# Norm products of the odd graphs moved from ScalarE to GpSimd, and the lists of the first and last slots in another order

## The chip, the cores and the metric

The kernel runs on one core of a Trainium2 chip. The metric is the device time of one execution in microseconds; before the change it was run three times. The five engines are TensorE (PE, matmuls; PEld its weight loads), VectorE (DVE), ScalarE (ACT), GpSimd (POOL) and SyncE (SP), which here issues all DMAs.

## The reference

Two layers act on 128 graphs of 128 nodes with 512 features each. Cut to what matters:

```python
# layer 0, 8 heads of 64
h = relu(layernorm(x))
m = h @ map_w.T + map_b
n = heads(m) / max(norm(heads(m)), 1e-8)
cos = n @ n.T                       # per head
keep_edge = cos > 0.1               # a 128 x 128 mask per head
q, k = heads(m @ q_w.T + q_b), heads(m @ k_w.T + k_b)
p = softmax(mask(q @ k.T / 8, adj))
a = keep_edge * p
x = x + relu((a @ heads(h @ gcn_map_w.T + gcn_map_b)) @ gcn_W.T / (a.sum(-1) + 1))
# layer 1, 4 heads of 64
h = relu(layernorm(x))
x = x + (softmax(mask(h@Wq @ (h@Wk).T / 8, adj)) @ (h@Wv)) @ Wo + bo
```

## The kernel before

The test `cos > 0.1` is made without a division: with N_i and N_j the norms of two nodes in one head, the product of m_i and m_j is compared with 0.1 N_i N_j. That second product, 8 heads of 128 x 128 in float32, is the tile `least`. It is built from `norm` (a column of norms for each head, with the 0.1 in it) and `norm_n` (the norms spread along the free dimension of all partitions by a DMA through `norm_d`). This work is called `threshold`. In the kernel before, ACT makes it with eight activations of 128 x 128 (L951), each with one column of `norm` as its scale; only for the very last graph GpSimd makes it in one instruction (`last_threshold`, L788). DVE then subtracts `least` from the cosines in PSUM (`above`, L1299), and after the exponentials sets to zero what is not above zero (`gate`, L1305).

All products are made in float16 pairs: a tile X is split into an upper part (ACT copies it to float16) and a lower part (POOL or DVE subtracts the upper part from X), and TensorE multiplies upper by upper, upper by lower and lower by upper. `e_upper`/`e_lower` do this for the attention weights of layer 0, `p1_lower` for the softmax weights of layer 1, `m_upper`/`m_lower`, `h1_upper`/`h1_lower` and so on for the others.

The work is a software pipeline over slots, one for each graph, written out by hand: each engine has its own list of calls for an odd slot and for an even slot, and special lists for the first slots (`n == 0`, `n == 1`, `n == 2`) and the last ones (called z, a, b, ... for graphs 125, 126, 127 and the slots after them). An engine runs its list strictly in order, and semaphores tie the lists together. In one slot different graphs are at different stages: slot n holds the scores of graph n, the features of n+1 or n+2, and layer 1 of the graphs n-1 to n-5. Two slots, an even one and an odd one, make a pair, after which the pattern repeats.

What stands around the change, in a pair of slots:

- ACT, even slot: `threshold(n)`, `scores_exp(n)` (eight exponentials with row sums, L940), `l1_exp` of one graph, `e_upper`, `m_upper`, `l1_exp` of another, `squares`, `v_upper` ("va"), `lv_upper`, `threshold(n+1)`, `h1_rows` and `h1_upper` (layer 1's normalised rows, L1007 and L1015), `v_upper` ("vb"). Odd slot: `x_rows` (L1022 and L1027), `scores_exp`, `o1_upper`, `qk_upper` twice, `e_upper`, and so on to `h1_rows`, `h1_upper`.
- POOL, even slot: `h1_lower`, `v_lower`, `keep_row`, `block_mask`, `result_base` (L715), `p1_lower` (L728), `e_lower` (L733), `m_lower` (L796), `p1_lower`, `norm_l1` (the reciprocal root and the shift of layer 1's normalisation, last instruction L809, for which `h1_rows` waits), `norm_l0` (the same of layer 0 for two graphs, last instruction L822, for which `x_rows` waits). Odd slot: `x_lower`, `o1_lower` (L722), `norm_rows` (L782), `e_lower`, `result_base`, `norm_l1` and others.
- DVE, odd slot: `scores_mask` (L1282, and the row maxima L1292 for which `scores_exp` waits), `above`, `gate`, then `o1_rows` (L1416), which frees the PSUM bank into which TensorE writes the next layer 1 queries (`lqk_part`, matmuls at L1903 with `w_lq`).

The first slots also split layer 1's four weights: ACT makes the upper parts (`l1_weights_upper`, L1165), DVE the lower ones (`l1_weights_lower`, L1711), and TensorE waits for them with `lw_done` before their first use.

Of the kernel before, what the change touches and what calls it, by code (L numbers as in the profile page):

```python
# [170 lines left out]
def build(nc, x, adj, map_w, map_b, q_w, q_b, k_w, k_b, gcn_map_w, gcn_map_b, gcn_W, Wq, Wk, Wv, Wo, bo, out):  # L171
# [15 lines left out]
    with ExitStack() as ctx:  # L187
# [494 lines left out]
        def _(pool):  # L682
# [101 lines left out]
            def last_threshold(s):  # L784

                pool.wait_ge(norm_in[1], 16 * (B // 2))
                pool.wait_ge(lowered, B - 1)
                nc.gpsimd.tensor_tensor(least[:, :, :], norm_n[:, 1].rearrange("p n h -> p h n"),  # L788
                                        norm[:, H:2 * H].unsqueeze(2).broadcast_to([P, H, P]),
                                        ALU.mult).then_inc(threshold_done, 1)  # L790
# [33 lines left out]
            def slot(s):  # L824
# [16 lines left out]
                elif s.n == 0:  # L841
                    v_lower(s)
                    keep_row(s)
                    block_mask(s)
                    m_lower(s)
                    norm_l0(s)
                    e_lower(s)
                elif s.n == 2:
                    h1_lower(s)
                    m_lower(s)  # L850
                    v_lower(s)
                    keep_row(s)
                    block_mask(s)
                    e_lower(s)
                    norm_l1(s)
                    norm_l0(s)
                else:
                    h1_lower(s)
                    v_lower(s)
                    keep_row(s)  # L860
                    block_mask(s)
                    result_base(s)
                    p1_lower(s, 4)
                    e_lower(s)
                    m_lower(s)
                    p1_lower(s, 3)
                    norm_l1(s)
                    norm_l0(s)
# [26 lines left out]
            e_lower(z)  # L895
            norm_l1(z)
            o1_lower(z, 4)
            result_base(z)
            v_lower(a)
            keep_row(a)  # L900
            last_threshold(b)
# [31 lines left out]
        def _(act):  # L933
# [141 lines left out]
            def slot(s):  # L1075
# [14 lines left out]
                elif s.n == 0:  # L1090
                    m_upper(s)
                    squares(s)
                    l1_weights_upper(0)
                    threshold(s)
                    scores_exp(s)
                    l1_weights_upper(1)
                    e_upper(s)
                    v_upper(s, "va", 2)
                    v_upper(s, "vb", 3)
                    threshold(Slot(s.n + 1, None, B))  # L1100
                    l1_weights_upper(2)
                    l1_weights_upper(3)
                elif s.n == 2:
                    m_upper(s)
                    squares(s)
                    threshold(s)
                    scores_exp(s)
                    e_upper(s)
                    v_upper(s, "va", 2)
                    threshold(Slot(s.n + 1, None, B))  # L1110
# [3 lines left out]
                else:  # L1114
# [9 lines left out]
                    threshold(Slot(s.n + 1, None, B))  # L1124
# [95 lines left out]
            threshold(a)  # L1220
# [47 lines left out]
        def _(dve):  # L1268
# [232 lines left out]
            def first_slot(s):  # L1501
# [4 lines left out]
                square_rest(s)  # L1506
                v_features(s, "va", 0)
                x_stats(s)
                above(s)
                gate(s)  # L1510
                v_features(s, "vb", 1)

            def slot(s):
# [3 lines left out]
                if s.n == 2:  # L1517
                    m_features(s, 0)
                    m_features(s, 1)
                scores_mask(s)  # L1520
                if s.odd:
# [4 lines left out]
                    if s.n == 1:  # L1526
                        norm_sums(s)
                        l1_weights_lower(0)
                        l1_weights_lower(1)
# [4 lines left out]
                    attended(s)  # L1534
                    k_features(s, 0)
# [6 lines left out]
                    result(s)  # L1542
                else:
                    l1_mask(s, 4)
                    l1_max(s, 4)
                    if s.n == 2:
                        l1_weights_lower(2)
                        l1_weights_lower(3)
                    else:
                        m_features(s, 0)  # L1550
# [4 lines left out]
                    if s.n > 2:  # L1555
                        m_features(s, 1)
# [230 lines left out]
            result(z)  # L1787
            gate(a)
            attended(a)
            x1_stats(a)  # L1790
            above(b)
# [53 lines left out]
        def _(pe):  # L1845
# [238 lines left out]
            def l1_values(s):  # L2084
                if s.has(-4):
                    ps = start_unit(s, "lv")
# [4 lines left out]
            def lqk_part(s, name, w):  # L2091
                if s.has(-3):
                    if s.n == 3:
                        pe.wait_ge(lw_done, len(st_l))
# [168 lines left out]
```

## Time and profile before

| | |
|---|---|
| median of 3 runs | 2642.72 us (2641.1 to 2645.03) |
| the profiled execution's own time | 2642.56 us |
| its span, first to last instruction | 2640.8 us |
| mean granted TensorE clock | 0.986 of full speed |
| busy: PE, DVE, ACT, POOL | 94%, 81%, 81%, 75% |
| HBM traffic over the span | 67 GB/s |

A line of a timeline has the start and the duration in us, the engine, the line of the kernel, the operation, the tiles out<-in, and in brackets the idle time of the engine just before and what ended it. Where several instructions of one kind follow each other, they stand in one line with their count and the time from the first's start to the last's end. 78086 instructions ran; the pairs of slots take about 40 us each and look alike from 160 us on.

### The profile page before, as it was taken

The numbers are of one execution on the slowest core, as the hardware profiler recorded it, in microseconds if no ns is written. First come the engines' busy times: TensorE is split into PE (matmuls) and PEld (weight loads), VectorE is DVE, ScalarE is ACT, GpSimd is POOL, SyncE is SP. The second block draws the span as 40 slices with busy tenths as digits, with TensorE's granted clock in tenths as the row PEclk, the third lists the DMA queues.
The fourth block names the chain that finished last, engine by engine and source line by source line (L and its number), as shares of the span: only waits on it lengthen the run. The fifth ranks groups of instructions, "written<-read, shape, count | busy, mean of one in ns | idle before, by whom it ended". The sixth has DMA issues, their size and how long they took to land.

```text
span 2640.8 us, 78086 instructions
## 1 busy us (share of the span) xinstructions
PE 2484.8 (94%) x29624; PEld 1981.5 (75%) x29624; DVE 2131.1 (81%) x3490; ACT 2147.2 (81%) x5544; POOL 1981.2 (75%) x2195
## 2 busy tenths in 40 slices
PE   7799999999999999999999999999999999999997
PEld 6677777777777777777777777777777777777775
DVE  6778787887888888787887878888887878878886
ACT  6787887887887877877878878878878878778776
POOL 3677777777777777777777777777777777777775
PEclk9899999999999999999999999999999999999999
DMA  6567677667676667667667677676776676776763
GB/s 162 115 115 149 139 136 150 136 140 150 134 141 147 133 143 146 129 143 146 128 146 142 134 149 138 138 150 135 139 147 131 141 148 128 147 146 128 144 130 72
DMA packets 855925, 364.05 MB, mean 138 GB/s; under 512 B 781440, under 2 KB 789120, under 8 KB 855552
## 3 DMA queue, kind: packets, MB, share of 16 engines
q1 hardware_dynamic: 855552, 359.06, 66.8%
q8 instruction: 236, 3.87, 0.6%
q14 instruction: 137, 1.12, 0.2%
HBM read 142.91 MB, written 34.08 MB: 67 GB/s over the span
## 4 chain that ended last, share of the span: by engine, by line
ACT 53%; issue 21%; POOL 15%; PE 8%; DVE 2%; DMA 1%; ACTq 0%; SPq 0%; POOLq 0%; DVEq 0%
ACT least L951 15%; ACT e_ec L940 13%; PE unit_ps L1903 5%; ACT p_sb L938 5%; POOL e_ec L733 4%; POOL qk_hl L754 4%; ACT h_sb L1007 4%; ACT v_sb L987 3%; ACT e_ec L980 2%; ACT m_hl L1064 2%; POOL x L715 2%; PE unit_ps L2075 2%; ACT h_hl L1027 2%; ACT xa L1022 2%; ACT sq_hl L1054 2%
## 5 line engine op out<-in xcount | busy, mean ns | idle before, releaser
L951 ACT ACTIVATE least<-norm_n,norm 128x128 f32<-128x128 f32 x1016 | 437.9, 515 | 3.0 <-DMA norm_n<-norm_d 3.0
L940 ACT ACTIVATE e_ec<-e_ec,neg_mx 128x128 f32<-128x128 f32 x1008 | 389.8, 388 | 4.1
L1046 ACT ACTIVATE qk_hl<-qk_sb 128x512 f16<-128x512 f32 x256 | 153.3, 622 | 276.9 <-DVE qk_sb L1341 276.9
L2075 PE MATMUL unit_ps<-m_hl,w_q_hi 128*128 128x256 f16 x2048 | 358.2, 274 | 0.0
L2075 PE MATMUL unit_ps<-m_hl,w_k_hi 128*128 128x256 f16 x2048 | 355.6, 272 | 2.6 <-DVE qk_sb L1341 2.6
L1305 DVE SCALAR_TENSOR_TENSOR e_ec<-c_ps,e_ec 128x1024 f32<-128x1024 f32 x126 | 154.3, 1225 | 237.5 <-ACT e_ec L940 235.7
L1903 PE MATMUL unit_ps<-h_t,w_m_hi 128*128 128x256 f16 x2048 | 341.2, 274 | 4.1 <-DVE qk_sb L1341 3.1
L1917 PE MATMUL unit_ps<-w_v_hi,h_t 128*128 128x512 f16 x1024 | 325.1, 379 | 0.0
L728 POOL TENSOR_TENSOR p_hl<-p_sb,p_hl 128x512 f16<-128x512 f32 x128 | 148.4, 1160 | 213.8 <-ACT p_hl L973 213.8
L733 POOL TENSOR_TENSOR e_ec<-e_ec 128x1024 f16<-128x1024 f32 x126 | 296.6, 2354 | 11.4 <-ACT e_ec L980 8.8
L1903 PE MATMUL unit_ps<-h_t,w_lq_hi 128*128 128x256 f16 x1024 | 197.0, 297 | 106.5 <-DVE o_sb L1416 105.4
L1903 PE MATMUL unit_ps<-h_t,w_m_lo 128*128 128x256 f16 x1024 | 279.9, 273 | 0.0
L709 POOL TENSOR_TENSOR h_hl<-h_sb,h_hl 128x512 f16<-128x512 f32 x128 | 148.8, 1162 | 142.7 <-ACT h_hl L1015 142.7
L2075 PE MATMUL unit_ps<-m_hl,w_q_lo 128*128 128x256 f16 x1024 | 238.5, 273 | 0.0
L2075 PE MATMUL unit_ps<-m_hl,w_k_lo 128*128 128x256 f16 x1024 | 237.3, 272 | 0.0
L2075 PEld LDWEIGHTS unit_ps<-m_hl,w_q_hi 128*128 128x128 f16 x2048 | 200.7, 98 | 29.2 <-issue 0.4
L1903 PEld LDWEIGHTS unit_ps<-h_t,w_m_hi 128*128 128x128 f16 x2048 | 195.8, 98 | 33.0 <-issue 4.4
L2075 PEld LDWEIGHTS unit_ps<-m_hl,w_k_hi 128*128 128x128 f16 x2048 | 200.2, 98 | 25.7 <-issue 2.8
L1365 DVE TENSOR_TENSOR qk_hl<-qk_sb,qk_hl 128x512 f16<-128x512 f32 x128 | 180.6, 1411 | 45.8 <-ACT qk_hl L1046 45.8
L1903 PEld LDWEIGHTS unit_ps<-h_t,w_lq_hi 128*128 128x128 f16 x1024 | 104.9, 106 | 140.8 <-issue 120.5
L1917 PE MATMUL unit_ps<-w_v_lo,h_t 128*128 128x512 f16 x512 | 194.0, 379 | 0.0
L940 ACT ACTIVATION_READ_ACCUMULATOR e_ec<-e_ec,neg_mx 128x1 f32 x1008 | 188.2, 187 | 0.0
(275 smaller groups left out, 7533.4 us busy)
## 6 DMA issues: line engine op xcount, KB each, us to landing
norm_n<-norm_d SPq DMA_DIRECT2D x128, 512.0 KB, 4.9
xa<-in_x_dram SPq DMA_DIRECT2D x128, 256.0 KB, 3.2
x<-in_x_dram SPq DMA_DIRECT2D x128, 256.0 KB, 2.9
out_dram<-x SPq DMA_DIRECT2D x128, 256.0 KB, 2.7
h_t<-h_hl SPq DMA_TRANSPOSE x254, 3.2
ec_t<-e_ec SPq DMA_TRANSPOSE x252, 3.4
adj_in<-in_adj_dram SPq DMA_DIRECT2D x128, 16.0 KB, 2.2
p_t<-p_hl SPq DMA_TRANSPOSE x126, 3.3
```

What stands on the lines that cost most here:

```text
L709: nc.gpsimd.tensor_tensor(h1_hl[:, a, 1, :], h1_sb[:, a, :], h1_hl[:, a, 0, :], ALU.subtract).then_inc(h1_lo, 1)
L728: nc.gpsimd.tensor_tensor(p1_hl[:, b, 1], p1_sb[:, b], p1_hl[:, b, 0], ALU.subtract).then_inc(p1_lo, 1)
L733: nc.gpsimd.tensor_tensor(e_hl[:, 1], e_of(s), e_hl[:, 0], ALU.subtract).then_inc(e_lo, 1)
L938: ins = nc.scalar.activation(e[:, h, :], e[:, h, :], ACT.Exp, bias=neg[:, h:h + 1], scale=SCALE)
L940: ins = nc.scalar.activation(e[:, h, :], e[:, h, :], ACT.Exp, bias=neg[:, h:h + 1], scale=SCALE, accum_out=sums[:, h:h + 1])
L951: ins = nc.scalar.activation(least[:, h, :], norm_n[:, g, :, h], ACT.Copy, scale=norm[:, g * H + h:g * H + h + 1])
L1046: nc.scalar.activation(dst[:, 0, c, :], src[:, c, :], ACT.Copy).then_inc(done, 1)
L1305: nc.vector.scalar_tensor_tensor(out=e_of(s), in0=c_ps[:, :, :].rearrange("p a (b n) -> p (a b) n", b=4), scalar=0.0, in1=e_of(s), op0=ALU ...
L1365: nc.vector.tensor_tensor(k_hl[:, 1, c, :], k_sb[:, c, :], k_hl[:, 0, c, :], ALU.subtract).then_inc(k_lo, 1)
L1903: ins = nc.tensor.matmul(out, w[a][:, i, c * P:(c + 1) * P], h[:, :, b, i, :], start=n == 0, stop=n == len(passes) - 1)
L1917: ins = nc.tensor.matmul(ps, h[:, a, i, :], w[b][:, i, :], start=n == 0, stop=n == len(passes) - 1)
L2075: ins = nc.tensor.matmul(ps[:, c % 2 * 2 * P:(c % 2 + 1) * 2 * P], w[a][:, i, c * P:(c + 1) * P], parts[:, b, i, :], start=n == 0, stop=n ...
```

## The change

The function `last_threshold` of GpSimd becomes `threshold(s)`, for any graph, with the waits that ACT's has: for the spread norms, for the norms themselves, and for `lowered`, that is until DVE has subtracted the previous graph's `least` (there is only one such tile). GpSimd calls it in each even slot for the next, odd graph, between `result_base` and `p1_lower`; ACT's calls for odd graphs go. The even graphs stay on ACT. Besides, the lists of slots 0, 1, 2, 3 and of the last graphs are put in another order on ACT, DVE and GpSimd, the splits of layer 1's weights are spread over slots 0 to 3, and TensorE waits for each of these weights only where it is used. In the last graphs GpSimd also makes the product of graph 126 (a).

```diff
-            def last_threshold(s):
-
-                pool.wait_ge(norm_in[1], 16 * (B // 2))
-                pool.wait_ge(lowered, B - 1)
-                nc.gpsimd.tensor_tensor(least[:, :, :], norm_n[:, 1].rearrange("p n h -> p h n"),
-                                        norm[:, H:2 * H].unsqueeze(2).broadcast_to([P, H, P]),
+            def threshold(s):
+
+                g = s.n % 2
+                pool.wait_ge(norm_in[g], s.at(lambda t: 16 * (t // 2 + 1)))
+                pool.wait_ge(norm_done, s.at(lambda t: t // 2 + 1))
+                pool.wait_ge(lowered, s.at(lambda t: t))
+                nc.gpsimd.tensor_tensor(least[:, :, :], norm_n[:, g].rearrange("p n h -> p h n"),
+                                        norm[:, g * H:(g + 1) * H].unsqueeze(2).broadcast_to([P, H, P]),
                                         ALU.mult).then_inc(threshold_done, 1)
...
                     m_lower(s)
                     norm_l0(s)
+                    threshold(Slot(s.n + 1, None, B))
                     e_lower(s)
...
                     result_base(s)
+                    threshold(Slot(s.n + 1, None, B))
                     p1_lower(s, 4)
...
             e_lower(z)
+            threshold(a)
             norm_l1(z)
             o1_lower(z, 4)
             result_base(z)
+            threshold(b)
             v_lower(a)
             keep_row(a)
-            last_threshold(b)
...
                 elif s.n == 0:
+                    threshold(s)
                     m_upper(s)
+                    scores_exp(s)
                     squares(s)
+                    e_upper(s)
                     l1_weights_upper(0)
-                    threshold(s)
-                    scores_exp(s)
                     l1_weights_upper(1)
-                    e_upper(s)
                     v_upper(s, "va", 2)
                     v_upper(s, "vb", 3)
-                    threshold(Slot(s.n + 1, None, B))
...
                     squares(s)
                     v_upper(s, "va", 2)
                     lv_upper(s)
-                    threshold(Slot(s.n + 1, None, B))
                     h1_rows(s)
                     h1_upper(s)
...
             lqk_upper(z, "lq", lq_hl, LQ)
-            threshold(a)
             scores_exp(a)
...
                 scores_mask(s)
-                square_rest(s)
+                above(s)
                 v_features(s, "va", 0)
                 x_stats(s)
-                above(s)
                 gate(s)
+                square_rest(s)
                 v_features(s, "vb", 1)
+                l1_weights_lower(0)
...
             scores_mask(b)
-            result(z)
             gate(a)
             attended(a)
             x1_stats(a)
+            result(z)
...
-                        pe.wait_ge(lw_done, len(st_l))
+                        pe.wait_ge(lw_done, 2 if name == "lq" else 3)
```

Of DVE's lists of slots 1 to 3 this is the order after the change: in slot 1 the keys' features come before `attended` and no weight is split; in slot 2 one weight is split between the two halves of `m_features` and one between `above` and `gate`, and `attended` comes ahead of `above`; in slot 3 the last weight is split ahead of `gate`.

**GpSimd in an even slot of the middle.** `v_sb` is layer 0's values, `x` the residual, `p_hl` the softmax weights of layer 1. Before:

```order
L739 TENSOR_TENSOR v_sb<-v_rows_sb,v_sb 128x8x64 x2
L763 TENSOR_SCALAR keep<-adj_in,v_unkept,v_unscale 128x1
L772 TENSOR_SCALAR block<-adj_in 128x128
L715 TENSOR_TENSOR x<-x,bias_o 128x512
L728 TENSOR_TENSOR p_hl<-p_sb,p_hl 128x512
L733 TENSOR_TENSOR e_ec<-e_ec 128x1024
```

and now:

```order
L739 TENSOR_TENSOR v_sb<-v_rows_sb,v_sb 128x8x64 x2
L763 TENSOR_SCALAR keep<-adj_in,v_unkept,v_unscale 128x1
L772 TENSOR_SCALAR block<-adj_in 128x128
L715 TENSOR_TENSOR x<-x,bias_o 128x512
L790 TENSOR_TENSOR least<-norm_n,norm 128x1024
L728 TENSOR_TENSOR p_hl<-p_sb,p_hl 128x512
L733 TENSOR_TENSOR e_ec<-e_ec 128x1024
```

One instruction, the product for the odd graph, stands between the residual's and the first subtraction of the softmax weights.

**ACT at the end of the same even slot and in the odd slot behind it.** Before:

```order
L998 ACTIVATE lv_sb<-unit_ps,v_scale 128x8x64
L951 ACTIVATE least<-norm_n,norm 128x128 x8
L1007 ACTIVATE h_sb<-x,shift,rstd 128x512
L1015 ACTIVATE h_hl<-h_sb 128x512
L987 ACTIVATE v_sb<-v_rows_sb 128x8x64
L1022 ACTIVATE xa<-xa,shift,rstd 128x512 x2
```

and now:

```order
L1004 ACTIVATE lv_sb<-unit_ps,v_scale 128x8x64
L1013 ACTIVATE h_sb<-x,shift,rstd 128x512
L1021 ACTIVATE h_hl<-h_sb 128x512
L993 ACTIVATE v_sb<-v_rows_sb 128x8x64
L1028 ACTIVATE xa<-xa,shift,rstd 128x512 x2
```

The eight activations of the odd graph are gone, and `h1_rows` (`h_sb`) follows `lv_upper` at once.

**ACT in slot 0.** `w_o_hi` and `w_lq_hi` are upper parts of layer 1's weights, the L940 group the exponentials. Before:

```order
L1064 ACTIVATE m_hl<-m_sb 128x1024
L1054 ACTIVATE sq_hl<-m_sb 128x1024
L1055 ACTIVATE sq_t<-m_sb 128x1024
L1165 ACTIVATE w_o_hi<-h_sb,scale 128x1024
L951 ACTIVATE least<-norm_n,norm 128x128 x8
L960 ACTIVATE neg_mx<-mx 128x8
L940 ACTIVATE e_ec,row_sum<-e_ec,neg_mx 128x128 x8
L1165 ACTIVATE w_lq_hi<-x,scale 128x1024
L980 ACTIVATE e_ec<-e_ec 128x1024
```

and now:

```order
L957 ACTIVATE least<-norm_n,norm 128x128 x8
L1070 ACTIVATE m_hl<-m_sb 128x1024
L966 ACTIVATE neg_mx<-mx 128x8
L946 ACTIVATE e_ec,row_sum<-e_ec,neg_mx 128x128 x8
L1060 ACTIVATE sq_hl<-m_sb 128x1024
L1061 ACTIVATE sq_t<-m_sb 128x1024
L986 ACTIVATE e_ec<-e_ec 128x1024
L1168 ACTIVATE w_o_hi<-h_sb,scale 128x1024
L1168 ACTIVATE w_lq_hi<-x,scale 128x1024
```

The product of graph 0 comes first, and the exponentials stand ahead of the squares and the weights. The SP queue's list is the same as before, and so is the number of matmuls.

## Rows read from the trace of the kernel before

**Rows 1.** The page's first section, busy time of each engine.

```profile
PE 2484.8 (94%) x29624; PEld 1981.5 (75%) x29624; DVE 2131.1 (81%) x3490; ACT 2147.2 (81%) x5544; POOL 1981.2 (75%) x2195
```

**Rows 2.** The waits between 400 and 2200 us: total us, times, longest us.

```profile
PE unit_ps L1903 <- DVE o_sb L1416: 80.2, 45, 2.1
```

**Rows 3.** The timeline of PE: start, duration us, then idle before and releaser.

```profile
1003.04 0.38 PE L1903 MATMUL unit_ps<-h_t,w_lq_hi 128*128 128x256 f16 x2 [2.07 <-DVE o_sb L1416]
...
1042.99 0.38 PE L1903 MATMUL unit_ps<-h_t,w_lq_hi 128*128 128x256 f16 x2 [2.07 <-DVE o_sb L1416]
...
1082.96 0.38 PE L1903 MATMUL unit_ps<-h_t,w_lq_hi 128*128 128x256 f16 x2 [2.08 <-DVE o_sb L1416]
...
1123.38 0.38 PE L1903 MATMUL unit_ps<-h_t,w_lq_hi 128*128 128x256 f16 x2 [0.89 <-DVE o_sb L1416]
```

**Rows 4.** The windows: span, busy us by engine, granted clock, DMA share, GB/s.

```profile
1084.00:1088.00 4.00, 4.00 (x25) 3.01 (x23) 3.67 (x7) 1.19 (x2) 4.00 (x3) 0.63 1.00 219
```

**Rows 5.** The timeline of ScalarE (ACT) over one pair of slots.

```profile
1012.88 0.81 ACT L1007 ACTIVATE h_sb<-x,shift,rstd 128x512 f32<-128x512 f32 x1 [1.10 <-POOL shift L809]
...
1029.94 3.45 ACT L951 ACTIVATE least<-norm_n,norm 128x128 f32<-128x128 f32 x8
...
1033.29 0.81 ACT L1007 ACTIVATE h_sb<-x,shift,rstd 128x512 f32<-128x512 f32 x1
...
1035.18 1.50 ACT L1022 ACTIVATE xa<-xa,shift,rstd 128x512 f32<-128x512 f32 x2
...
1037.63 0.19 ACT L960 ACTIVATE neg_mx<-mx 128x8 f32<-128x8 f32 x1
...
1040.95 0.40 ACT L1038 ACTIVATE o_hl<-o_sb 128x256 f16<-128x256 f32 x1
```

**Rows 6.** The timeline of GpSimd (POOL) over the same pair.

```profile
1018.54 1.27 POOL L715 TENSOR_TENSOR x<-x,bias_o 128x512 f32<-128x512 f32 x1
...
1023.17 1.16 POOL L728 TENSOR_TENSOR p_hl<-p_sb,p_hl 128x512 f16<-128x512 f32 x1 [3.35 <-ACT p_hl L973]
...
1030.96 1.04 POOL L809 TENSOR_TENSOR shift<-nm,rstd 128x1 f32<-128x1 f32 x1
...
1033.48 0.20 POOL L822 TENSOR_TENSOR shift<-nm,rstd 128x2 f32<-128x2 f32 x1
...
1041.42 0.67 POOL L722 TENSOR_TENSOR o_hl<-o_sb,o_hl 128x256 f16<-128x256 f32 x1 [1.86 <-ACT o_hl L1038]
```

**Rows 7.** The timeline of VectorE (DVE) over the same pair.

```profile
1018.60 1.22 DVE L1299 TENSOR_TENSOR c_ps<-c_ps,least 128x1024 f32<-128x1024 f32 x1
...
1030.74 1.22 DVE L1431 SCALAR_TENSOR_TENSOR sq_hl<-sq_hl,sq_t 128x1024 f16<-128x1024 f16 x1
...
1033.78 1.22 DVE L1292 TENSOR_REDUCE mx<-e_ec 128x8 f32<-128x1024 f32 x1
...
1041.07 1.23 DVE L1305 SCALAR_TENSOR_TENSOR e_ec<-c_ps,e_ec 128x1024 f32<-128x1024 f32 x1 [3.08 <-ACT e_ec L940]
```

**Rows 8.** The groups of POOL by line: busy us, mean ns, idle before.

```profile
L788 POOL TENSOR_TENSOR least<-norm_n,norm 128x1024 f32<-128x1024 f32 x1 | 2.4, 2428 | 0.0
```

**Rows 9.** The timelines of ACT, SP, DVE and POOL in the first slots.

```profile
57.06 1.06 ACT L1064 ACTIVATE m_hl<-m_sb 128x1024 f16<-128x1024 f32 x1 [7.37 <-DVE m_sb L1341]
...
47.23 0.80 SPq L568 DMA_DIRECT2D norm_n<-norm_d  x2
...
60.96 3.42 ACT L951 ACTIVATE least<-norm_n,norm 128x128 f32<-128x128 f32 x8
...
98.92 2.14 DVE L1711 SCALAR_TENSOR_TENSOR w_lv_lo<-p_sb,scale,w_lv_hi 128x1024 f16<-128x1024 f32 x1
...
97.88 4.17 POOL L739 TENSOR_TENSOR v_sb<-v_rows_sb,v_sb 128x512 f16<-128x512 f32 x2
```

**Rows 10.** The page's section on DMA issues: KB each, us to landing.

```profile
norm_n<-norm_d SPq DMA_DIRECT2D x128, 512.0 KB, 4.9
```

**Rows 11.** The timeline of ACT in the last graphs.

```profile
2573.30 3.46 ACT L951 ACTIVATE least<-norm_n,norm 128x128 f32<-128x128 f32 x8 [3.01 <-DMA norm_n<-norm_d]
```

More of the change, by code:

```diff
@@ L862, in slot @@
                     result_base(s)
+                    threshold(Slot(s.n + 1, None, B))
                     p1_lower(s, 4)
@@ L1104, in slot @@
                     m_upper(s)
-                    squares(s)
                     threshold(s)
                     scores_exp(s)
+                    squares(s)
                     e_upper(s)
                     v_upper(s, "va", 2)
-                    threshold(Slot(s.n + 1, None, B))
                     h1_rows(s)
@@ L1123, in slot @@
                     lv_upper(s)
-                    threshold(Slot(s.n + 1, None, B))
                     h1_rows(s)
@@ L1518, in slot @@
                     m_features(s, 0)
+                    l1_weights_lower(1)
                     m_features(s, 1)
@@ L1527, in slot @@
                         norm_sums(s)
-                        l1_weights_lower(0)
-                        l1_weights_lower(1)
+                    elif s.n == 3:
+                        l1_weights_lower(3)
                     gate(s)
@@ L1533, in slot @@
                         norm_sums(s)
-                    attended(s)
-                    k_features(s, 0)
+                        attended(s)
+                        k_features(s, 0)
+                    else:
+                        k_features(s, 0)
+                        attended(s)
                     x1_stats(s)
@@ L1542, in slot @@
                     result(s)
+                elif s.n == 2:
+                    attended(s)
+                    x1_stats(s)
+                    above(s)
+                    l1_weights_lower(2)
+                    gate(s)
+                    v_features(s, "va", 0)
+                    x_stats(s)
+                    square_rest(s)
+                    v_features(s, "vb", 1)
                 else:
@@ L1545, in slot @@
                     l1_max(s, 4)
[L1546 to L1550, printed above, removed]
+                    m_features(s, 0)
                     l1_mask(s, 3)
@@ L1554, in slot @@
                     l1_max(s, 3)
-                    if s.n > 2:
-                        m_features(s, 1)
+                    m_features(s, 1)
                     attended(s)
@@ L2085, in l1_values @@
                 if s.has(-4):
+                    if s.n == 4:
+                        pe.wait_ge(lw_done, len(st_l))
                     ps = start_unit(s, "lv")
```

## The prediction

> **What bounds the kernel now.** The page first: PE is busy 94% of the span, the others 75 to 81% [rows 1], so at most 6% can come from TensorE's waits. The table of waits says where they are: in 45 pairs of slots between 400 and 2200 us TensorE waits 80.2 us in all before the layer 1 queries, for DVE's `o_sb` [rows 2], and nothing else of size holds it. The timeline of PE shows one pair: queries start at 1003.04 and again at 1042.99, a pair of 39.95 us, and the wait is 2.07 us [rows 3]. In one pair of four the granted clock falls just behind that wait (0.63 over 4 us [rows 4]); that pair takes 1123.38 - 1082.96 = 40.42 us, its wait 0.89 us [rows 3]. Mean: (3 x 39.95 + 40.42) / 4 = 40.07 us.
>
> Now follow the wait back. `o_sb` stands on DVE behind `gate`, which starts at 1041.07 after idling 3.08 us for ACT's exponentials [rows 7]. ACT ends them as `o_hl` starts, 1040.95, and from `h_sb` at 1012.88 to there its rows follow each other without idle time; `h_sb` had waited 1.10 us for POOL's `shift` [rows 5]. And POOL's shift ends a stretch of work that began with `o_hl`, right behind the previous exponentials (at 1041.42 in this pair [rows 6]). So the loop is ACT for 28.1 us (1012.88 to 1040.95) and POOL for the other 11.9. TensorE is not in it: it needs 39.95 - 2.07 = 37.88 us.
>
> **The change, the pairs in the middle.** Removed from ACT: `least` of the odd graph at 1029.94, after which `h_sb` comes at 1033.29, so 3.35 us [rows 5]. This is not what the loop gains. `h_sb` needs POOL's `shift` of this slot, which starts at 1030.96 and takes 1.04 us, to 1032.00 [rows 6]; so `h_sb` can move from 1033.29 to 1032.04, by 1.25 us. The next row that needs POOL, `xa`, would move from 1035.18 to 1033.93 [rows 5], and its input, the second `shift`, ends at 1033.68 [rows 6]: no further wait. `neg_mx` moves from 1037.63 to 1036.38; the maxima it needs are there at 33.78 + 1.22 = 1035.00 [rows 5, 7]. The exponentials, `gate`, `o_sb` and the queries follow by the same 1.25 us. TensorE's wait shrinks to 2.07 - 1.25 = 0.82 us: it stays second. **1.25 us a pair**, a pair of 38.70.
>
> Added to POOL: one product. Its only row before is 2.43 us [rows 8], made in the last graphs while DVE works. It may start when `x` ends, 18.54 + 1.27 = 1019.81, and when `above` has let go of `least`, 18.60 + 1.22 = 1019.82 [rows 6, 7]. So it ends at 1022.25, in the 3.35 us that POOL idles for ACT's `p_hl`, until 1023.17 [rows 6]. Cover left: 0.92 us. Behind it POOL has no idle time up to the second `shift`, so anything over 0.92 us would move both shifts, one for one. Bounds of its price: below, twice `p_hl`, which has half the elements and takes 1.16 us [rows 6]: 2.3; above, its own row plus the most that I see POOL held up: two `v_sb` of that half size took 4.17 us instead of 2.3 beside DVE's weight splits [rows 9], so 2.43 + 1.87 = 4.30. I take 2.43, its own row. At 4.30 it would run 4.30 - 2.43 - 0.92 = 0.95 us past its cover, and 0.30 of the 1.25 us would be left.
>
> Could the product slow DVE? What DVE runs in its time is `gate`, which reads PSUM and one SBUF tile. In the odd slot `gate` takes 1.23 us beside POOL's `o_hl` from 1041.42 on [rows 6, 7], as everywhere. So no. The product itself goes into the same tile in the same form; SP's list is unchanged, and `spread_norms` waits for products that are now done earlier.
>
> How many pairs: even slots 4 to 122 give the full 1.25 us, 60 of them: 75.0 us. In the last even slot (124) there is no `xa` in the way before and the exponentials already stand against the maxima: nothing.
>
> **The first slots.** ACT idles 7.37 us before 57.06 and then works without a break until slot 1's exponentials are done. Product 0, 3.42 us, goes ahead of that into the idle time: its norms were sent at 47.23 [rows 9] and land some 4.9 us later [rows 10], so it ends near 55.5. Product 1 goes to POOL's idle time. That is 2 x 3.3 = 6.6, less 1.3 that ACT now idles for the maxima of slot 0: 5.3. Behind, slots 2 and 3 have one weight split where two stood between maxima and `above` (to 98.92 + 2.14 [rows 9]), worth up to 4 on DVE, of which I count 1.7, since TensorE needs 5 to 6 us of matmuls there anyway. Together **7 us**; bounds 3.3 (one product only) and 10.6 (both, and both splits). TensorE's wait for weights moves later and costs nothing: each is split two matmul groups before its use.
>
> **The last graphs.** ACT's product of graph 126 started at 2573.30, when the norms landed, and took 3.46 [rows 11]. On POOL it starts at the same landing and takes 2.43: **1 us**. Behind it on POOL wait `norm_l1`, `o1_lower` and `result_base` of slot z, some 3 us later than before; ACT's `h_rows` then stand behind its exponentials anyway. `result` leaves the front of `gate` and loses it 0.65. Bounds 0 and 2.3.
>
> **Sum.** 75.0 + 7 + 1 = 83 us off the profiled execution's own 2642.56 us gives 2559.6; the median of the runs is 0.16 above that execution, so **2560 us**.
>
> The Trainium skill (GPSIMD Engine Reference, Engine selection) speaks against such a move: elementwise work belongs on VectorE, GpSimd being about twice as slow for two inputs. The trace agrees on the ratio: 2.43 us here against 1.22 for DVE's `above` of the same size [rows 7, 8]. But the engine that is relieved is ACT, which takes 3.45. By the rule the product would go to DVE, in its idle time before `gate`, and the sum would be the same: the loop's 1.25 us come from ACT's list alone.
>
> **Rivals.**
>
> A. *The collision behind the shift goes away* (6%). `shift` takes 1.04 us at 1030.96, the like one of layer 0 only 0.20 [rows 6]; it ends with DVE's `square_rest`, 1030.74 to 1031.96 [rows 6, 7]. If new timing parts the two, POOL is 0.84 us earlier and TensorE becomes the bound: all 2.07 us, 60 x 2.07 = 124, with the rest 132: 2510 us. Against it: both hang on rows ahead of the removed one (`p_hl`, `squares`, `lv_sb`), which keep their distances. The Trainium skill (SBUF — State Buffer, Who interferes with whom) has this as a lock: a DVE instruction with two SBUF inputs and a GpSimd one that reads SBUF exclude each other for a whole instruction; the trace agrees at this row.
>
> B. *POOL is late* (14%). The product is held up, or starts late because `above` does. Between 0.92 and 2.17 us of delay eat the 1.25. At the upper price, 4.30, the pairs give 60 x 0.3 = 18 and the whole comes to 2642.7 - 26 = 2617; half way to the forecast, 2588. For it: the 4.17 of the first slots. Against it: in those pairs DVE runs nothing with two SBUF inputs in that stretch.
>
> C. *Slower* (3%). The same place, one mechanism: from 0.92 + 1.25 = 2.17 us over its row, that is a product of over 4.60 us, POOL takes over the loop, and every further microsecond counts 60 times. At twice its row, 4.86 us, it is 0.26 x 60 = 16 less the 8 of both ends: 2651 us. It needs more than the upper price.
>
> D. *The change does nothing in the middle* (3%): another wait behind the exponentials that I have not seen, with only the ends gained: 2635 us.
>
> E. *The clock* (within the forecast). A shorter wait may let the clock fall more often than once in four pairs. Each such pair costs the loop 0.47 us; twice as often is 15 x 0.47 = 7 us, 2567.
>
> **How the numbers follow.** The forecast with E has 74%, between 2545 and 2572. The range reaches to half of B, 2590, and down to 2540, which leaves out A (6%) and the worse part of B, C and D (12%). A difference under 0.2% (5.3 us) is about what a measurement of this kernel can't tell from none. Faster: all but C, and a part of D: 0.94; same 0.03; slower 0.03.
>
> **What would show it.** Right: pairs of 38.7 us, TensorE's wait before the queries near 0.8 us, ACT idling some 2.1 us before `h_sb` in the even slot for `shift`, the product in POOL's row at 2.4 us with idle time left behind it before `p_hl`. Wrong: no such idle time on ACT but a wait of POOL's `p_hl` gone (B, C); a `shift` of 0.2 us in the even slot and a TensorE without a wait (A); queries of slot 3 less than 4 us earlier than now (first slots).

## The result, and the profile after

The median after is **2556.4 us** (2554.0 to 2557.2, 4 runs), beside 2643.1 us (2641.1 to 2645.0) for the kernel before, run alongside: a ratio of **0.967, interval 0.9654 to 0.9687**, faster by 87 us. The profiled execution has a span of 2555.3 us (before 2640.8), and its mean granted clock is 0.994 (before 0.986).

The page's first section answers to [rows 1]: ACT has given 207 us of busy time, POOL has taken 149, and TensorE is busy for 96% instead of 94%.

```profile
PE 2460.2 (96%) x29624; PEld 1967.7 (77%) x29624; DVE 2142.0 (84%) x3490; ACT 1940.6 (76%) x5032; POOL 2130.0 (83%) x2259
```

The waits between 400 and 2200 us of the kernel after, to be held against [rows 2] (total us, times, longest):

```profile
PE unit_ps L1915 <- DVE o_sb L1418: 38.2, 46, 0.8
```

The same place in the timeline of PE, against [rows 3]: one pair is 1045.47 - 1006.75 = 38.72 us.

```profile
1006.75 0.38 PE L1915 MATMUL unit_ps<-h_t,w_lq_hi 128*128 128x256 f16 x2 [0.83 <-DVE o_sb L1418]
...
1045.47 0.38 PE L1915 MATMUL unit_ps<-h_t,w_lq_hi 128*128 128x256 f16 x2 [0.83 <-DVE o_sb L1418]
```

The timelines of POOL, DVE and ACT in that pair, against [rows 5 to 7]:

```profile
1022.24 1.27 POOL L715 TENSOR_TENSOR x<-x,bias_o 128x512 f32<-128x512 f32 x1
1023.70 2.46 POOL L790 TENSOR_TENSOR least<-norm_n,norm 128x1024 f32<-128x1024 f32 x1 [0.18 <-DVE c_ps L1301]
1026.89 1.16 POOL L728 TENSOR_TENSOR p_hl<-p_sb,p_hl 128x512 f16<-128x512 f32 x1 [0.72 <-ACT p_hl L979]
...
1034.68 1.04 POOL L811 TENSOR_TENSOR shift<-nm,rstd 128x1 f32<-128x1 f32 x1
```

```profile
1034.46 1.22 DVE L1433 SCALAR_TENSOR_TENSOR sq_hl<-sq_hl,sq_t 128x1024 f16<-128x1024 f16 x1
...
1043.55 1.22 DVE L1307 SCALAR_TENSOR_TENSOR e_ec<-c_ps,e_ec 128x1024 f32<-128x1024 f32 x1 [1.84 <-ACT e_ec L946]
```

```profile
1035.75 0.81 ACT L1013 ACTIVATE h_sb<-x,shift,rstd 128x512 f32<-128x512 f32 x1 [2.00 <-POOL shift L811]
```

The product lies in POOL's old idle time and leaves 0.72 us of it. ACT, 3.35 us lighter, now stands 2.00 us before `h_sb` for POOL's `shift`. `shift` still takes 1.04 us beside DVE's `square_rest`, and `gate` waits 1.84 us instead of 3.08: 1.24 us have gone out of the pair.

The windows from 480 to 2400 us, first of the kernel before and then of the one after (span, busy us by engine, granted clock, DMA share, GB/s):

```profile
480.00:2400.00 1920.00, 1835.97 (x22036) 1465.41 (x22035) 1569.77 (x2543) 1584.90 (x4113) 1478.80 (x1630) 0.99 0.69 140
```

```profile
480.00:2400.00 1920.00, 1879.06 (x22816) 1505.46 (x22813) 1629.88 (x2629) 1483.51 (x3882) 1646.24 (x1737) 1.00 0.74 145
```

Before, 16 of the 59 pairs between the queries of slots 5 and 123 are the slowed ones of 40.42 us [rows 3, 4]. After, none is: 53 of the 55 pairs that lie between 200 and 2400 us take 38.7 us, and the longest of all 39.0. The 0.63 of [rows 4] is the mean of 4 us. Within them TensorE runs at half its clock, 1.2 GHz, for 3 us and more (kernel before, same columns):

```profile
1084.00:1087.00 3.00, 3.00 (x16) 2.13 (x14) 2.96 (x7) 0.63 (x1) 3.00 (x2) 0.50 1.07 245
```

**The account of the 85.5 us of span**, by the starts of the layer 1 queries in both timelines. Those of slot 5 move from 161.10 to 154.53 us, 6.6 earlier: 1.25 of it is the pair that slot 4 belongs to, 5.3 are the first slots. From there to the queries of slot 123 there are 59 pairs: 2365.0 us before, 2284.7 after, 80.3 less, which is 59 x 1.24 = 73 and 16 x 0.46 = 7 for the slowed pairs. From slot 123's queries to the end it is 114.7 us before and 116.0 after, 1.4 more. 6.6 + 80.3 - 1.4 = 85.5. The two end terms are those of one pair of traces: with the same new first slots and the old middle (experiment 2) slot 5's queries are 3.4 us earlier than before, and with the old first slots and the new middle (experiment 1) 0.3 us.

### The profile page after: what moved, and what is told of

The parts are those of the page before. It is cut to its first block, busy times and chain, and to the rows that moved or that the text cites. A ratio compares the mean times of both kernels' runs of the same rounds, so it can differ in the third digit from the quotient of the medians.

```text
span 2555.3 us, 77639 instructions
## 1 busy us (share of the span) xinstructions
PE 2460.2 (96%) x29624; PEld 1967.7 (77%) x29624; DVE 2142.0 (84%) x3490; ACT 1940.6 (76%) x5032; POOL 2130.0 (83%) x2259
## 4 chain that ended last, share of the span: by engine, by line
PE 76%; POOL 7%; ACT 7%; issue 4%; DVE 3%; DMA 1%; SPq 1%; ACTq 0%; DVEq 0%; POOLq 0%
PE unit_ps L1915 22%; PE unit_ps L1929 21%; PE unit_ps L2087 21%; PE s_ps L1939 3%; PE s_ps L1992 3%; PE c_ps L1939 3%; ACT e_ec L946 3%; POOL e_ec L733 2%; PE unit_ps L2059 1%; ACT least L957 1%; PE unit_ps L1939 1%; POOL p_hl L728 1%; POOL qk_hl L754 1%; DVE o_sb L1418 1%; PE unit_ps L2003 1%
## 5 line engine op out<-in xcount | busy, mean ns | idle before, releaser
L1013 ACT ACTIVATE h_sb<-x,shift,rstd 128x512 f32<-128x512 f32 x128 | 104.1, 814 | 196.3 <-POOL shift L811 196.3
L1367 DVE TENSOR_TENSOR qk_hl<-qk_sb,qk_hl 128x512 f16<-128x512 f32 x128 | 193.7, 1513 | 45.8 <-ACT qk_hl L1052 45.8
L1915 PE MATMUL unit_ps<-h_t,w_lq_hi 128*128 128x256 f16 x1024 | 171.0, 272 | 50.7 <-DVE o_sb L1418 49.8
L957 ACT ACTIVATE least<-norm_n,norm 128x128 f32<-128x128 f32 x504 | 217.2, 514 | 2.1 <-DMA norm_n<-norm_d 2.0
```

Source lines behind the costliest of these rows:

```text
L957: ins = nc.scalar.activation(least[:, h, :], norm_n[:, g, :, h], ACT.Copy, scale=norm[:, g * H + h:g * H + h + 1])
L1367: nc.vector.tensor_tensor(k_hl[:, 1, c, :], k_sb[:, c, :], k_hl[:, 0, c, :], ALU.subtract).then_inc(k_lo, 1)
L1915: ins = nc.tensor.matmul(out, w[a][:, i, c * P:(c + 1) * P], h[:, :, b, i, :], start=n == 0, stop=n == len(passes) - 1)
```

## The experiments

**1 and 2. The two halves apart.** The first kernel is the one before with the middle's edit alone. The second is the changed one with that edit undone. The first one's diff, POOL's list and then ACT's in the even slots from 4 on (the function is that of the change):

```diff
                     result_base(s)
+                    threshold(Slot(s.n + 1, None, B))
                     p1_lower(s, 4)
...
                     lv_upper(s)
-                    threshold(Slot(s.n + 1, None, B))
                     h1_rows(s)
```

> The kernel before, with the one edit of the middle: in the even slots from 4 on the odd graph's product is made on POOL and no longer on ACT; first slots and last graphs keep their old lists. My working: 60 pairs x 1.25 us = 75, and the 15 pairs that the falling clock lengthened by 0.47 us each are gone too, 7: 82 us under the kernel before, 2561 us, pairs of 38.71 us, TensorE's wait 0.83 us. Rival 1, the clock's 7 us come from the new lists of the ends and not from the shorter wait: some pairs are still slowed and the time is 2568. Rival 2, the first slots' new order also feeds the middle: pairs longer than 38.9 us and a time above 2573.

> The changed kernel with the middle undone: from slot 4 on the odd graph's product is on ACT again, between lv_sb and h_sb; the new lists of the first slots and of the last graphs stay. My working: the first slots give 6.6 us and the last graphs cost 1.3, so 5 us under the kernel before, 2638 us; pairs of 39.95 us with a wait of 2.07 us on TensorE, and again about one pair in four at 40.42. Rival, the fall of the clock depends on how the first slots leave it and not on the wait: no slowed pairs, 2631 us.

Measured: the middle alone **2561.1 us**, ratio 0.969 (0.9681 to 0.9708); the ends alone **2638.3 us**, ratio 0.998 (0.9974 to 0.9992). Against 2642.2 these are 81 and 4 us, together 85 of the 87. The ends alone are 0.2% faster, clear of the noise but small. Experiment 1 has no slowed pair between its slots 5 and 123 (pairs of 38.71 us, the longest 38.87); experiment 2 has them as before, one in four at 40.4 us behind waits of 2.07. So the clock's 7 us come with the middle's edit, and neither rival holds.

**3. `result` of slot 125.** At the end of the kernel after, the timeline of PE shows a wait that the one before did not have, and the timeline of DVE what it waited for:

```profile
2497.45 0.39 PE L1929 MATMUL unit_ps<-w_lv_hi,h_t 128*128 128x256 f16 x1 [3.01 <-DVE x L1477]
```

```profile
2492.32 1.22 DVE L1307 SCALAR_TENSOR_TENSOR xa<-c_ps,xa 128x1024 f32<-128x1024 f32 x1
...
2496.65 0.75 DVE L1477 SCALAR_TENSOR_TENSOR x<-unit_ps,y_scale,x 128x512 f32<-128x512 f32 x1 [0.28 <-issue]
```

```diff
             scores_mask(b)
+            result(z)
             gate(a)
             attended(a)
             x1_stats(a)
-            result(z)
             above(b)
```

> The changed kernel with result of slot 125 back in front of gate of graph 126 on DVE, where it stood before. My theory: behind x1_stats it holds a matmul bank that TensorE's values of layer 1 need, and TensorE waits 3.01 us for it; in front it frees the bank in time, gate of graph 126 is 0.65 us later, and the time falls by 1 to 3 us, to 2553 to 2555. Rival: gate's 0.65 us and the exponentials behind it hold TensorE just as long, and the time stays at 2556 or rises by up to 0.7 us.

Measured: **2554.1 us**, ratio 0.966 (0.965 to 0.9676). The wait of 3.01 us is gone from the trace. From slot 125's queries to the end it is 71.2 us, against 75.7 in the kernel after and 73.3 to 75.4 in the nine other kernels with the new lists of the ends; experiment 9, the one other with `result` in front, has 71.8. The old lists have 74.3 (kernel before) and 72.4 (experiment 1). So the traces show some 2 to 3 us for this placement. Part of that is the clock: in the kernel after it is 0.50 from 2495.3 to 2502.0 us, in experiment 3 from 2495.4 to 2498.7 us only, and 1.00 behind. The medians, whose intervals overlap, do not settle it.

**4. `square_rest` behind.** `shift` and `square_rest` are to be parted by exchanging two neighbours on DVE:

```diff
                     lv_lower(s)
-                    square_rest(s)
                     v_features(s, "vb", 1)
+                    square_rest(s)
```

> The changed kernel with square_rest and v_features vb exchanged on DVE in the even slots from 4 on, so that square_rest starts some 0.7 us later, when POOL's shift of layer 1 (0.20 us of work) has begun and ended by itself. Theory of the collision (rival A of the prediction): shift takes 0.2 instead of 1.04 us, ACT's h_sb starts 0.84 us earlier, TensorE's wait of 0.83 us is gone and it is the bound: pairs of 37.9 us, 60 x 0.83 = 50 us less, 2506 us. Rival 1, the lock only moves: square_rest now falls on the rstd or shift of layer 0, xa is as late as before, and pairs stay at 38.7 us, 2556. Rival 2, the norm sums wait for square_rest's result, which is 0.7 us later: TensorE waits there instead, up to 0.7 us a pair, so 42 us of the 50 are lost.

Measured: **2550.4 us**, ratio 0.965 (0.9638 to 0.9664); pairs of 38.6 us. The timelines of POOL and of DVE in this kernel:

```profile
1033.37 0.19 POOL L811 TENSOR_TENSOR shift<-nm,rstd 128x1 f32<-128x1 f32 x1
1033.74 0.19 POOL L819 TENSOR_SCALAR ve<-mv 128x2 f32<-128x2 f32 x1 [0.19 <-issue]
1034.02 1.08 POOL L820 TENSOR_SCALAR nm<-mv 128x2 f32<-128x2 f32 x1
```

```profile
1033.80 1.22 DVE L1433 SCALAR_TENSOR_TENSOR sq_hl<-sq_hl,sq_t 128x1024 f16<-128x1024 f16 x1
```

`shift` takes 0.19 us, but now `nm` of layer 0 takes 1.08 instead of 0.23 (in this pair; the median is 1.19): it too ends with `square_rest`, at 1035.1. ACT's `xa` waits for that chain (0.62 us). It is rival 1: the hold-up has moved on by two instructions, and 0.1 us a pair is what is won, not the 0.83 of the theory.

**5. The norm steps ahead of the second `p1_lower`.**

```diff
                     m_lower(s)
-                    p1_lower(s, 3)
                     norm_l1(s)
                     norm_l0(s)
+                    p1_lower(s, 3)
```

> The changed kernel with both norm steps (norm_l1, norm_l0) ahead of the second p1_lower on POOL in the even slots from 4 on, instead of behind it; DVE's order as in the changed kernel. Theory: the loop is POOL's chain up to the shifts, and 1.16 us of it (that p_hl) need not be in it. ACT's xa can then start 0.80 us earlier, where DVE's v_rows_sb becomes its limit; TensorE's wait of 0.83 us goes: pairs of 37.9 us, about 50 us less than the changed kernel, 2507 us. Rival 1: that p_hl ends some 2.7 us later, its transpose too, and TensorE waits for it before the layer 1 values; each 0.1 us of such a wait costs 6 us. Rival 2: square_rest meets the layer 0 steps instead and holds one for up to 1.0 us: xa is then still 1.1 us earlier on POOL's side, and nothing changes in the time.

Measured: **2516.6 us**, ratio 0.953 (0.9514 to 0.954), 40 us below the kernel after (expected: 50). TensorE has no wait for `o_sb` any more and is busy 1789 of the 1800 us between 400 and 2200; two thirds of the pairs take 37.7 or 38.0 us. Both rivals hold in part. The second `shift` still meets `square_rest` (0.52 instead of 0.20 us), without effect. And the later transpose is sometimes late, in pairs of 38.6 to 38.8 us. TensorE's waits between 400 and 2200 us:

```profile
PE unit_ps L2059 <- DMA p_t<-p_hl: 5.8, 7, 0.9
PE unit_ps L2087 <- DVE qk_sb L1343: 2.7, 6, 0.8
```

**6. Past the cover.** The product is made twice.

```diff
                     result_base(s)
+                    product(Slot(s.n + 1, None, B))
                     threshold(Slot(s.n + 1, None, B))
```

> The changed kernel with the product on POOL made twice in each even slot from 4 on (same tile, same result), to test what lies past its cover. Theory of rival C in the prediction: the second 2.46 us has 0.72 us of idle time left before p_hl, so both shifts move by 1.8 us, one for one: pairs of 40.5 us, 61 x 1.8 = 110 us more, 2666 us, and with a wait of 2.6 us on TensorE the clock falls as before, some 7 us more: 2673. Rival: moved by 1.8 us, the shift no longer meets square_rest and takes 0.2 instead of 1.04 us, which gives back 0.84: pairs of 39.7 us, 61 x 0.96 = 59 more, 2615 us.

Measured: **2691.9 us**, ratio **1.019** (1.0173 to 1.0201). The timeline of POOL; no idle time is left between the rows:

```profile
1033.57 2.46 POOL L791 TENSOR_TENSOR least<-norm_n,norm 128x1024 f32<-128x1024 f32 x1 [0.20 <-DVE c_ps L1315]
1036.11 2.45 POOL L803 TENSOR_TENSOR least<-norm_n,norm 128x1024 f32<-128x1024 f32 x1
1038.51 1.17 POOL L729 TENSOR_TENSOR p_hl<-p_sb,p_hl 128x512 f16<-128x512 f32 x1
...
1045.06 1.05 POOL L819 TENSOR_SCALAR ve<-mv 128x1 f32<-128x1 f32 x1
```

The pairs take 40.50 us, 1.79 more, as rival C's working has it: past the cover, one for one, and slower than before. The rival of this run falls in the same way as experiment 4's theory: `shift` takes 0.19 us, but `ve` 1.05. And here DVE is held by POOL as well: `square_rest` takes 1.76 us instead of 1.22, since a `p_hl` is running on POOL (1043.81 to 1044.97) as it starts:

```profile
1044.30 1.76 DVE L1447 SCALAR_TENSOR_TENSOR sq_hl<-sq_hl,sq_t 128x1024 f16<-128x1024 f16 x1
```

About one pair in four is slowed again, and here such a pair takes 42.28 us, 1.78 more and not 0.46. That is the 19 us by which the time is above the expected 2673: from slot 5's queries to slot 123's it is 59 x 1.78 + 15 x 1.78 = 132 us more than in the kernel after, of 133 in all. The trace shows why a slowed pair costs so much more. At half the clock TensorE's matmuls delay DVE's `qk_sb`, and `above` with it, by 1.67 us, in the kernel before as here. There POOL's 3.35 us of idle time took that up. Here POOL has none left, its first product starts 1.67 us later, and the loop gets it all:

```profile
992.93 2.47 POOL L791 TENSOR_TENSOR least<-norm_n,norm 128x1024 f32<-128x1024 f32 x1 [1.39 <-DVE c_ps L1315]
```

TensorE's wait before the queries is 2.08 us and not the expected 2.6: up to 0.5 us of it is now a wait for `qk_sb`. Rival C's own figure does not hold: it has 2651 us for a product of 4.86 us, and this run is 41 us above that. Mainly, the cover was 0.2 us smaller (60 x 0.2 = 12), and C reckoned with no more for the slowed pairs than before (19).

**7, 10 and 12. How long a wait brings the clock down.** ACT gets 6, 12 or 15 of these where the product stood:

```diff
+            def idle_product(s, heads):
+                for h in range(heads):
+                    nc.scalar.activation(filled[:, h, :], filler[:, :], ACT.Copy, scale=1.0)
...
                     lv_upper(s)
+                    idle_product(s, 12)
                     h1_rows(s)
```

> The changed kernel with six one-head ACTIVATEs of a constant tile put on ACT in the even slots where the product stood (nothing reads their result): about 6 x 0.43 = 2.6 us, of which ACT's wait for shift covers 2.0. It asks how long TensorE's wait must be for its clock to fall. Working: pairs of 39.3 us and a wait of 1.4 us, 2556 + 61 x 0.6 = 2592 us. Theory 1, only the full 2.07 us bring the clock down: no slowed pairs, 2592. Theory 2, the falls come in proportion to the wait: some 10 slowed pairs at 0.47 us, 2597, and the mean clock of 480 to 2400 us is between 0.99 and 1.00.

> The changed kernel with twelve one-head ACTIVATEs of a constant tile on ACT where the product stood (nothing reads their result). Six took 1.29 us and were wholly covered; twelve should take 2.6 us, 0.5 us more than ACT's wait of 2.1, so pairs of 39.2 us and a wait of 1.3 us on TensorE: 2556 + 61 x 0.5 = 2587 us. Theory 1, the clock falls only behind a wait of about 2.07 us: no slowed pairs, 2587. Theory 2, it falls in proportion: some 8 to 10 slowed pairs of 0.5 to 1.8 us each, 2592 to 2603.

> The changed kernel with fifteen of the constant ACTIVATEs. Twelve took 2.49 us, made pairs of 39.01 us and a wait of 1.12 us on TensorE, and no pair was slowed; a wait of 2.07 us came with one slowed pair in four, whether ACT's product (the kernel before) or POOL's second product made it. Fifteen add 0.6 us: pairs of 39.6 us, a wait of 1.7 us. Theory 1, the wait's length alone decides and 1.7 us are still too short: no slowed pairs, 2575 + 61 x 0.6 = 2612 us. Theory 2, 1.7 us are long enough: slowed pairs as in the kernel before, one in four or fewer, at 0.5 us each: 2615 to 2619 us.

Measured: **2556.5**, **2575.1** and **2609.1 us**. Six were mis-sized by me: one took 0.21 us, not the 0.43 of a head of the product, so all lay within ACT's wait and the run tells only that this wait is free time. Twelve reach 0.3 us past it, not 0.5 (expected: 2587 us): the pairs are 39.01 us and TensorE's wait 1.12; with 15 they are 39.60 and 1.72:

```profile
1025.77 0.38 PE L1923 MATMUL unit_ps<-h_t,w_lq_hi 128*128 128x256 f16 x2 [1.72 <-DVE o_sb L1426]
```

```profile
480.00:2400.00 1920.00, 1837.63 (x22327) 1471.61 (x22327) 1594.32 (x2572) 1588.95 (x4515) 1614.17 (x1698) 1.00 0.69 142
```

Not one pair of experiment 12 is slowed (all from slot 7 on take 39.6 us), and the clock of the window is 1.00; nor is one of experiments 7 and 10. The slowed pairs are there in the three kernels with waits of 2.07 us (before, 2 and 6), whether ACT or POOL makes the wait, and in none with 1.72 or less. But the wait's length alone does not bring the clock down. In the kernel before, 28 of the 44 waits of about 2.07 us between slots 5 and 123 are followed by no fall, and neither is any of the 15 waits of 2.75 us that end experiment 6's slowed pairs. Nor do these runs part the wait's length from what changes with it, the length of the pair and TensorE's share of idle time in it. The window's busy times (1838 us in experiment 12, 1836 in the kernel before) are close only because the slowed matmuls of the kernel before take longer: it did 22036 matmuls in that time, against 22327. What decides which of the long waits brings a fall stays open.

**8. The product on DVE**, between `above` and `gate`:

```diff
                     above(s)
+                    threshold(Slot(s.n + 1, None, B))
                     gate(s)
                     l1_max(s, 3)
```

> The changed kernel with the odd graph's product of the even slots from 4 on made by DVE, between above and gate, where DVE idles 1.25 us for the exponentials, and not by POOL. The prediction says that the sum would be the same, since the 1.25 us a pair come from ACT's list alone: pairs of 38.7 us, 2556 us, if the product takes about 1.2 us on DVE as above does. Rival: in this form (read across heads, one factor repeated) it takes up to POOL's 2.46 us, gate is up to 1.2 us later, and what waits for the gated weights is late too: up to 60 x 1.2 = 72 us more, if that is on the path.

Measured: **2555.2 us**, ratio 0.967 (0.9658 to 0.9684), the same as on POOL. The timeline of DVE:

```profile
1023.46 1.22 DVE L1300 TENSOR_TENSOR c_ps<-c_ps,least 128x1024 f32<-128x1024 f32 x1
1024.82 2.02 DVE L1435 TENSOR_TENSOR least<-norm_n,norm 128x1024 f32<-128x1024 f32 x1
1026.75 1.22 DVE L1306 SCALAR_TENSOR_TENSOR e_ec<-c_ps,e_ec 128x1024 f32<-128x1024 f32 x1
```

It takes 2.02 us and not the 1.22 of `above`: 0.8 us more than `gate` had to idle. The pair is still 38.7 us, but it gets there another way. The rows above are from one of 6 pairs in which `square_rest` holds `shift` as in the kernel after; these take 39.2 to 39.7 us. In the other 53 `shift` takes 0.19 us and `ve` of layer 0 is held instead, for 1.24 us here:

```profile
1075.27 1.24 POOL L819 TENSOR_SCALAR ve<-mv 128x2 f32<-128x2 f32 x1
```

There ACT waits 0.68 us for `shift` and 0.45 us for DVE's `v_rows_sb`, and TensorE 0.33 us before the queries and 0.34 (median) for `qk_sb`. So the equal time is a meeting of two different limits, in part luck, and not the same limit again.

**9. Experiments 3 and 5 together**, with both their edits.

> The changed kernel with the two edits that paid, together: norm steps ahead of the second p1_lower (which took the time to 2516.6 us) and result of slot 125 back in front of gate of graph 126 (which took the changed kernel from 2556.4 to 2554.1). If they add up: 2514 us. Rival: in the faster kernel TensorE reaches the last graphs by another schedule, and result costs it as much in front as behind: 2517.

Measured: **2516.6 us** (2512.7 to 2520.1), ratio 0.9525, where experiment 5 has 0.9527. The last graphs are 2.2 us shorter in its trace, and the runs do not show it. It did not add up (expected 2514, rival 2517), or the step is smaller than the spread of the runs.

**11. `square_rest` with one SBUF input.**

```diff
-                    nc.vector.scalar_tensor_tensor(out=sq_hl[:, 1], in0=sq_hl[:, 0], scalar=-REST, in1=sq_t[:, :, :],
-                                                   op0=ALU.mult, op1=ALU.add).then_inc(sq_lo, 1)
+                    if s.n < 4:
+                        nc.vector.scalar_tensor_tensor(out=sq_hl[:, 1], in0=sq_hl[:, 0], scalar=-REST, in1=sq_t[:, :, :],
+                                                       op0=ALU.mult, op1=ALU.add).then_inc(sq_lo, 1)
+                    else:
+                        nc.vector.tensor_reduce(spare[:, :], sq_t[:, :, :].rearrange("p c (h n) -> p (c h) n", n=P), AX_X, ALU.max).then_inc(sq_lo, 1)
```

> The changed kernel with square_rest of the slots from 4 on replaced by a reduction of the same size, with one SBUF input instead of two, into a spare tile: the low half of the squares is left out of the norm sums. The reductions of this size take 1.22 us, as square_rest does, so nothing moves but the number of inputs. Theory of the lock: POOL's shift takes 0.2 instead of 1.04 us at the same place, all 0.84 us go to the loop, TensorE's wait of 0.83 us with it: pairs of 37.9 us, 2506 to 2510 us. This is rival A of the prediction. Rival, shift is slow for another reason (the trace draws it so, or it waits for the value of rstd): it still takes 1.04 us and the time stays at 2556.

Measured: **2512.0 us**, ratio 0.950 (0.9491 to 0.9516). The timelines of DVE and of POOL at this place:

```profile
1016.93 1.21 DVE L1438 TENSOR_REDUCE spare<-sq_t 128x8 f32<-128x1024 f32 x1
```

```profile
1017.15 0.19 POOL L812 TENSOR_TENSOR shift<-nm,rstd 128x1 f32<-128x1 f32 x1
```

`shift` lies in the middle of a DVE instruction of the same length and takes 0.19 us. 58 of the 59 pairs take 37.95 to 37.99 us and TensorE is busy 1916 of 1920 us: 44 us are gained. The edit takes away the second input, but also most of the output (128x8 elements instead of 128x1024). That the output is not the cause shows in the kernel after: `scores_mask` writes 128x1024 elements to SBUF, has one SBUF input (the other is in PSUM) and is as long, and POOL's second `shift` in the middle of it takes 0.19 us.

```profile
1036.25 1.21 DVE L1284 SCALAR_TENSOR_TENSOR e_ec<-adj_in,s_ps 128x1024 f32<-128x1024 uint8 x1
```

```profile
1037.19 0.19 POOL L824 TENSOR_TENSOR shift<-nm,rstd 128x2 f32<-128x2 f32 x1
```

## Why the prediction was right

The forecast was 2560 us, in a range of 2540 to 2590; it came to 2556.4. The mechanism is as forecast; that the total is only 3.6 us off is in part luck, since 7 us that it left out are set against 4 that it counted and that are not there. (The part that its range leaves out of B, C and D adds up to 13% and not 12.) By its steps:

- **ACT + POOL loop, 1.25 us a pair**: 1.24. The limit that it named, `shift` at `h_sb`, is ACT's new wait of 2.00 us; TensorE's wait is 0.83 us (forecast 0.82), a pair 38.71 (38.70). Experiment 1 shows the middle alone. Neither `xa` nor the maxima took any of it; experiment 2, the middle undone, has the old pairs of 39.95 us back.
- **The product's price and cover**: 2.46 us (2.43, the row of the last graphs), with 0.72 us of idle time left instead of 0.92, since the product starts 0.18 us after `above` ends and not at once. What is beyond the cover counts one for one (experiment 6), as rivals B and C have it; C's figure for a doubled product is 41 us too low (experiment 6). B, at 14%, rested on the 4.17 us of the first slots, and nothing of that kind happened in the middle.
- **60 pairs**: right, slots 4 to 122. The pair behind them, from slot 123's queries to slot 125's, gains nothing, as said: 40.33 us before and 40.32 after.
- **The first slots, 7 us won**: 5.3 in this pair of traces. The mark that it set itself, queries of slot 3 at least 4 us earlier, is missed: they are 3.1 us earlier. What is missing is as large as the term of 1.7 us for the weight splits, but that it is this term is not shown. The trace shows a collision that was not counted: as `square_rest` starts in slot 2, POOL's `e_lower` is running (until 103.72), and it takes 2.76 us, where the kernel before has 1.19; POOL's `ve` then takes 1.05 us beside it. Behind them `above` of slot 3 waits for POOL's product, and `w_lv_lo` stands ahead of `gate`:

```profile
102.04 2.76 DVE L1433 SCALAR_TENSOR_TENSOR sq_hl<-sq_hl,sq_t 128x1024 f16<-128x1024 f16 x1
...
110.27 1.23 DVE L1301 TENSOR_TENSOR c_ps<-c_ps,least 128x1024 f32<-128x1024 f32 x1 [1.76 <-POOL least L790]
112.07 2.23 DVE L1723 SCALAR_TENSOR_TENSOR w_lv_lo<-p_sb,scale,w_lv_hi 128x1024 f16<-128x1024 f32 x1
114.22 1.21 DVE L1307 SCALAR_TENSOR_TENSOR e_ec<-c_ps,e_ec 128x1024 f32<-128x1024 f32 x1
```

  Among kernels with the same new first slots those queries start between 114.6 and 119.0 us, so a term of 1 to 2 us is not told apart there.
- **The last graphs, 1 us won**: 1.4 us lost in this pair of traces; over all kernels the new lists average about 1 us more than the old. That `result` leaves the front of `gate` was counted as 0.65 us won. What waits for `result` itself was not looked for: it frees the bank of matmuls that come next, and TensorE stood 3.01 us (experiment 3). The traces show it; the size is at the edge of what the medians do.
- **The clock (rival E)**: the wrong sign. It reckoned with more falls behind a shorter wait. There are none, and these 7 us are the largest term that the sum lacked: with them and the two misses above it is 83 + 7 - 1.7 - 2.4 = 86. That they come with the middle's edit is shown (experiments 1 and 2); why no fall follows the shorter wait is not.
- **Rival A**: right that it would not happen by itself, right in its price (TensorE as the bound, 37.9 us a pair, 2510 us; experiment 11 has 2512), and shown as a mechanism by experiment 11. The Trainium skill (SBUF — State Buffer, Who interferes with whom) says that a DVE instruction with two SBUF inputs contends with a GpSimd one that reads SBUF; the trace agrees, with 1.04 us beside two inputs and 0.19 beside one. That new timing would part the two was too simple: experiments 4, 6 and 8 moved them, and a neighbour of `shift` was held instead.
- **DVE in POOL's place**: the same time, as said, though not at the stated price, nor, in 53 of 59 pairs, with the stated limit (experiment 8). By the Trainium skill (GPSIMD Engine Reference, Engine selection) GpSimd is about twice as slow at two inputs; for this product the traces show 2.46 against 2.02 us, so here the advantage is a fifth.

## What to carry to other kernels

Moving work off a loaded engine is worth the distance to the next limit (here 1.25 of 3.35 us), and that limit is the next thing to move: putting 1.16 us of POOL's work behind what ACT waited for gave another 40 us. Before an instruction is put later in a list, ask who waits for it, and not only who stands behind it. When two engines hold each other up at one place, a shift in time mostly hands the delay to a neighbour; taking away the shared input, or taking that chain off the path, removes it.

## What the hardware showed that was not expected

- The granted clock fell from 2.4 to 1.2 GHz behind some of the waits of 2.07 us (16 slowed pairs in the kernel before) and behind none of 1.72 us or less (experiments 7, 10 and 12). Most of the waits of 2.07 us, and all 15 of 2.75 us in experiment 6, brought no fall. The same fall cost 0.46 us where another engine's idle time covered the delay, and 1.78 us where there was none left.
- One DVE instruction of 1.22 us with two SBUF inputs stretched whichever of POOL's small norm steps met it: `shift` 0.19 to 1.04 us, `nm` 0.23 to 1.19, `ve` 0.19 to 1.05 and 1.24. It works the other way too: POOL's running instruction stretched `square_rest` from 1.22 to 1.76 us (experiment 6) and to 2.76 (first slots of the kernel after).
- The same product of 128x1024 elements, read across heads, takes 2.02 us on DVE, 2.46 on POOL and 3.45 on ACT (0.43 a head), while ACT does a copy of one contiguous 128x128 tile into half the width in 0.21 us.
